# GNN block on one core: node order phase, block, graph in the column tiles, normalisation on ScalarE, and an instruction sequence of its own for the first pair

## What is computed

```
h = max(layernorm(x), 0)
hc = h transposed to (graph, feature, node)
c = relu(bn1(conv1(hc)))                  # 128x128, one tap
c = bn2(conv2(c))                         # 17 taps along the nodes
x_conv = relu(c + hc) transposed back
s = h @ w_se.T + b_se                     # 3 features per node
A = exp(-|s_n - s_m|^2) * adj
msg = relu(h @ w_msg.T + b_msg)
x_nmp = A @ msg
gi = [x_conv, x_nmp] @ w_ih.T + b_ih ; gh = h @ w_hh.T + b_hh
r, z = sigmoid(gi_r + gh_r), sigmoid(gi_z + gh_z)
n = tanh(gi_n + r * gh_n)
out = x + (1 - z) * n + z * h
```

## Time and profile before

| | |
|---|---|
| median of 3 runs | 337.67 us (337.13 to 338.13) |
| the profiled execution, its own time | 337.86 us |
| its span, first to last instruction | 336.1 us |
| mean granted TensorE clock | 0.954 |
| busy: PE, DVE, ACT, POOL | 304.8, 277.2, 152.0, 29.7 us |

### The profile page before, as it was taken

How to read it: one execution, slowest core, us unless ns; L and a number is a source line. 1 busy time by engine, 2 the same in 40 slices (tenths; PEclk the granted TensorE clock), 3 DMA queues, 4 the chain that set the end, 5 groups by cost and what they waited for, 6 DMA issues and landing times.

```text
span 336.1 us, 5716 instructions
## 1 busy us (share of the span) xinstructions
PE 304.8 (91%) x2041; PEld 278.7 (83%) x2041; DVE 277.2 (82%) x654; ACT 152.0 (45%) x250; POOL 29.7 (9%) x35
## 2 busy tenths in 40 slices
PE   5808883989999999999999999999999999999991
PEld 4708773977999899989998899889998999899880
DVE  7999977389898989898989898998989896847345
ACT  1545532446454555285426543554545652730241
POOL 5733100010001000100001000100010000000000
PEclk9865998799999999999999999999999999999995
DMA  7902100070016000700062003400140002002002
GB/s 224 188 4 38 27 2 0 25 164 2 2 29 161 1 2 0 178 12 0 3 126 65 0 3 65 124 0 2 32 96 0 0 3 62 2 1 64 0 0 64
DMA packets 52144, 14.87 MB, mean 44 GB/s; under 512 B 34548, under 2 KB 51972, under 8 KB 51988
## 3 DMA queue, kind: packets, MB, share of 16 engines
q1 hardware_dynamic: 51518, 13.18, 16.9%
q10 hardware_dynamic: 438, 1.25, 1.2%
q0 software_dynamic: 160, 0.07, 0.4%
HBM read 10.30 MB, written 4.19 MB: 43 GB/s over the span
## 4 chain that ended last, share of the span: by engine, by line
PE 77%; DVE 3%; ACT 2%; issue 1%; DVEq 0%; ACTq 0%
PE bank L886 22%; PE bank L887 21%; PE bank L888 21%; PE bank L956 3%; PE bank L983 3%; PE bank L1039 2%; PE bank L931 2%; PE bank L975 1%; PE bank L966 1%; DVE stats L533 0%; DVE place L676 0%; ACT a_hi L371 0%; ACT edge L395 0%; DVE place L687 0%; ACT a_hi L374 0%
## 5 line engine op out<-in xcount | busy, mean ns | idle before, releaser
L886 PE MATMUL bank<-a_hi,w_hi 128*128 128x256 f32 (+1 forms) x328 | 100.3, 306 | 5.7 <-DVE place L676 5.7
L887 PE MATMUL bank<-a_lo,w_hi 128*128 128x256 f32 (+1 forms) x328 | 96.8, 295 | 0.0
L888 PE MATMUL bank<-a_hi,w_lo 128*128 128x256 f32 (+1 forms) x328 | 96.7, 295 | 0.0
L886 PEld LDWEIGHTS bank<-a_hi,w_hi 128*128 128x128 f32 x328 | 64.6, 197 | 6.5 <-issue 5.9
L887 PEld LDWEIGHTS bank<-a_lo,w_hi 128*128 128x128 f32 x328 | 64.5, 197 | 0.6
L888 PEld LDWEIGHTS bank<-a_hi,w_lo 128*128 128x128 f32 x328 | 64.2, 196 | 0.0
L306 POOL TENSOR_TENSOR rstd<-var_eps,halves 128x8 f32<-128x8 f32 (+1 forms) x9 | 13.6, 1511 | 208.2 <-DVE var_eps L550 208.2
L886 PE MATMUL bank<-h_hi,w_hi 128*128 128x512 f32 (+1 forms) x66 | 26.7, 405 | 1.5 <-DVE ms_b L599 1.3
L363 ACT ACTIVATE a_f<-bank,bn_shift,bn_scale 128x512 f32<-128x512 f32 x16 | 12.5, 785 | 30.6 <-PE bank L888 28.2
L887 PE MATMUL bank<-h_lo,w_hi 128*128 128x512 f32 (+1 forms) x66 | 25.5, 386 | 0.0
L888 PE MATMUL bank<-h_hi,w_lo 128*128 128x512 f32 (+1 forms) x66 | 25.4, 385 | 0.0
(11 more groups left out here) (142 smaller groups left out, 646.2 us busy)
## 6 DMA issues: line engine op xcount, KB each, us to landing
adj_in<-in_adj SPq DMA_DIRECT2D x64, 64.0 KB, 2.3
x_slot<-in_x SPq DMA_DIRECT2D x8, 256.0 KB, 4.0
place<-in_x SPq DMA_DIRECT2D x8, 256.0 KB, 3.9
out<-x_slot SPq DMA_DIRECT2D x8, 256.0 KB, 2.6
out<-place SPq DMA_DIRECT2D x7, 256.0 KB, 2.5
place<-in_L_gnn_conv_w ACTq DMA_DIRECT2D x1, 1088.0 KB, 7.1
place<-in_L_gnn_w_ih SPq DMA_DIRECT2D x1, 384.0 KB, 4.4
out<-place SPq DMA_DIRECT2D x2, 128.0 KB, 2.3
```

What stands on the lines that cost most here:

```text
L886: pe.matmul(out, w_hi[:, mat, :], hi, start=start, stop=False)
L887: pe.matmul(out, w_hi[:, mat, :], lo, start=False, stop=False)
L888: final = pe.matmul(out, w_lo[:, mat, :], hi, start=False, stop=stop)
```

## The change

It reorders the nodes: x is loaded in four DMAs for each half pair, so that partition r*32+v holds node 4v+r, and y is stored in four. A column tile stands now phase by phase, in a phase block (v) by block, and for each block its 4 graphs. A phase of a half pair is 128 columns in a row, and a shift by one block is a shift by 4 columns for all 4 graphs. In return, what belongs to one graph is every fourth column (`by_graph`): the banks that `h_transposes` and `aggregate` write, the weights that `messages` and `out_transposes` load. The adjacency rows are loaded four times, each time whole (2 KB pieces), at offsets 0 to 3, and `adj_transposed` reads every fourth element. The columns that only a rounding to even limits took in are no longer computed. `x_normed` moves to ACT with a bias that POOL makes, and `edge` shares the space of `x_norm`. `conv_out` is cut by half pair. The differences of taps move from POOL to DVE except for the last two, copies to ACT; vectors are loaded behind the big weight on ACT's queue. The first pair has its own order on PE, ACT and DVE. The last pair's transposes by graph need both column parts. In the diff, `x_normed` and `gates` are ACT's, and `first_pair` is DVE's.

```
         def load_x(s, k):
-            sp.dma_start(x_slots[s % 4][:, k * GB:(k + 1) * GB, :], ...).then_inc(x_in[s % 4][k], 16)
+            src = x[...].rearrange("b (v r) d -> r v b d", r=4)
+            for r in range(4):
+                sp.dma_start(x_slots[s % 4][r * VN:(r + 1) * VN, k * GB:(k + 1) * GB, :], src[r]
+                             ).then_inc(x_in[s % 4][k], 16)
...
         def load_adj(s, k):
-            for i in range(N // QUAD):
-                src = adj[..., :, rows].rearrange("b (j c) a -> c b j a", c=QUAD)
-                sp.dma_start(adj_in[k][rows, :, :].rearrange("c b (j a) -> c b j a", a=QUAD), src)
+            src = adj[...].rearrange("b (c r) m -> c b (r m)", r=4)
+            for i in range(4):
+                sp.dma_start(adj_in[k][i * QUAD:(i + 1) * QUAD, :, 3 - i:3 - i + 4 * N], src)
...
         def norm_rstd(i, graphs):
             pool.tensor_tensor(rstd[:, graphs], var_eps[:, graphs], halves[:, graphs], ALU.pow)
+            pool.tensor_tensor(norm_bias[:, graphs], neg_mean[:, graphs], rstd[:, graphs], ALU.mult)
...
+            def x_normed(s, k):
+                act.wait_ge(nbias_ready, (k if s == 0 else s + 1) + 1)
+                if k == 0:
+                    wait(act, edgem_ready, 2 * s)
+                for b in range(k * GB, (k + 1) * GB):
+                    act.activation(x_norm[:, b, :], x_slots[s % 4][:, b, :], ACT.Identity,
+                                   bias=norm_bias[:, b:b + 1], scale=rstd[:, b:b + 1])
...
-                dve.transpose(adj_T[k][:, :], adj_in[k][:, :, :].rearrange("n b m -> n (b m)"))
+                dve.transpose(adj_T[k][:, :].rearrange("m (b n) -> m b n", b=GB), adj_in[k][:, :, 3:3 + 4 * N:4])
...
-                    lo = max(0, begin - shift) // 2 * 2
-                    hi = min(VN, (VN - shift + 1) // 2 * 2)
+                    lo, hi = max(0, begin - shift), min(VN, VN - shift)
...
+            def by_graph(ap):
+                return ap[:, :].rearrange("p (n b) -> p b n", b=GB)
             def h_transposes(t, k):
-                    tr = pe.transpose(bank[B_F[k]][:, b * N:(b + 1) * N], x_norm[:, k * GB + b, :], ident[:, :])
+                    tr = pe.transpose(by_graph(bank[B_F[k]])[:, b], x_norm[:, k * GB + b, :], ident[:, :])
...
                     for b in range(b0, b1):      # messages
-                                      h_f[p][:, b * N:(b + 1) * N], w_ms[:, :], start=True, stop=True)
+                                      by_graph(h_f[p][:, half(b // GB)])[:, b % GB], w_ms[:, :], ...)
...
             def distances(t, k):
-                pe.wait_ge(msb_ready, 3 * t + 3 - k)
+                if t == 1:
+                    pe.wait_ge(b_added, 1)
+                    pe.wait_ge(convf_ready, 4)
...
+            def gates(s):
+                gate_r(s, 0)
+                gate_z(s, 0)
+                x_normed(s + 2, 0)
+                gate_n(s, 0)
+                x_normed(s + 2, 1)
+                hh_n_half(s, 1)
...
+            def first_pair():
...
+                vector_columns()
+                odd_differences(0)
+                first_differences()
+                norm_columns()
+                second_differences()
+                h_low(0, 0)
+                weights_low(1)
+                h_low(0, 1)
+                weights_low(2)
+                messages(0)
+                phase_sums(0)
+                weights_low(3)
+                dist_sides(0)
+                a1_low_sums(0)
...
```

More of the change, by code:

```diff
@@ L467, in iteration @@
                     h_copies(t, 1)
[L468 to L473 removed]
+                gate_n(s - 1, 1)
+                g_scaled(s)
                 if ahead:
@@ L496, in iteration @@
                     nmp_high(t, 1)
-                gate_r(s, 0)
-                gate_z(s, 0)
-                gate_n(s, 0)
-                hh_n_half(s, 1)
-            for s in range(NP):
+                gates(s)
+            first_pair()
+            gates(0)
+            nmp_high(1, 0)
+            nmp_high(1, 1)
+            for s in range(1, NP):
                 iteration(s)
@@ L686, in conv_out @@
                     dve.wait_ge(comb_f, 2)
[L687 to L688 removed]
+                to = conv_f[:, half(k)].rearrange("p (q e w) -> p e q w", q=2, e=2)[:, e]
+                product, rest = (ap.rearrange("p (q k w) -> p k q w", q=2, k=2)[:, k]
+                                 for ap in (bank[B_CB][:, :], pre[e]))
+                dve.scalar_tensor_tensor(to, product, bn_scale[:, 1:2], rest, ALU.mult, ALU.add
+                                         ).then_inc(convf_ready, 1)
             def conv_low(s, k):
@@ L852, in iteration @@
                 if ahead:
-                    a1_low(t)
+                    a1_low_sums(t)
+                    a1_low_phases(t)
                     nmp_low(t, 1)
-                n_hidden(s, 0)
-                n_argument(s, 0)
-                z_times_h(s, 0)
-                if s + 2 < NP:
-                    x_normed(s + 2, 0)
-                z_times_n(s, 0)
-                gates_out(s, 0)
-                if s + 2 < NP:
-                    x_normed(s + 2, 1)
-            for s in range(NP):
+                gates(s)
+            first_pair()
+            gates(0)
+            nmp_low(1, 0)
+            nmp_low(1, 1)
+            for s in range(1, NP):
                 iteration(s)
@@ L1097, in _ @@
-            pe.transpose(bank[B_Z][:, 0:NVEC], vecs[:, :], ident[0:NVEC, 0:NVEC]).then_inc(vecT_done, 1)
-            h_transposes(0, 1)
-            weight_transposes(1)
-            pe.wait_ge(w_ms_ready, 2)
-            messages(0)
-            split_done(1)
-            conv1(0, 0)
-            conv1(0, 1)
-            weight_transposes(2)
-            weight_transposes(3)
-            dist_transposes(0)
-            weight_transposes(4)
-            distances(0, 0)
-            distances(0, 1)
```

627 lines of the change are left out of this document (348 added, 279 removed).

## The result

The changed kernel takes 347.29 us (median of 4 runs, 346.33 to 348.06) beside 337.90 for the kernel before on the same chip (337.13 to 338.75): a ratio of 1.028, 95% interval 1.024 to 1.032. I had forecast 329.4 us and a faster kernel. The profiled execution is the one of 348.06 us, with a span of 346.1.

The account below looks back on a forecast made before the run. PE was taken to bound the iterations, with the gain to be won in the first 83 us. 337.86 - 8.8 (first pair) + 0.5 (ACT behind) - 1.3 (iterations) + 1.3 (end) gave 329.6, median 329.4; range 325 to 336.8.

Parts of the forecast that it names:

- PE's own access: PE's weight loads and bank writes at every fourth float32: taken as 0, upper bound 5.1 us a pair.
- rival (2): PE pays for loads and writes at 16-byte steps, up to 361 us; chance of slower 0.13, of 333 to 337 0.08.
- Leg 1: Startup up to the first product "g": vectors at 9.6, then 15.7 us of DVE, so "g" starts at 25.3.
- Rival (3): Startup held by data: vectors and big weight land 3 us or more later, 332.5 to 336 us; chance 0.11.
- Leg 2: Startup from "g" at 25.3 to pair 1's transposes at 41.0, through DVE, POOL's rstd and ACT's normalisation.
- Leg 3: PE's work from pair 1's transposes at 41.0, priced by columns: 15.9 us, to 56.9.
- Leg 4: Gates of pair 0, up to pair 2's first transpose: at 74.6, where it was 83.43 before.
- Iterations: Pairs bound by PE: fewer columns save 0.18 us a pair, 1.3 over seven pairs; 35.5 us from iteration to iteration.
- ACT's cover for the normalisation: In the iterations ACT takes 2.0 us more, hidden ahead of hh_n; without cover each pair pays up to 2 us.
- The end: Last results and stores: transposes wait for both parts (0.4), eight issues at 0.26 or less; 1.3 us more.
- The startup: The first pair, up to pair 2's first transpose: 8.8 us shorter than before, 74.6 where it was 83.43.

Follow-up runs that it names:

- e1: The changed kernel, but messages loads 128 neighbouring columns of h_f as weights and not every fourth: 332.99 us, ratio 0.983.
- e2: The kernel before, but messages loads every fourth column of h_f (16 bytes apart) as weights: 351.07 us, ratio 1.037.
- e3: The changed kernel, but h_transposes and aggregate write their 128 columns side by side in the bank: 348.36 us, ratio 1.029.
- e6: e4 with vectors back on SP's queue behind x, ahead of the adjacency, and conv2's weights behind w_se on ACT's: 340.70 us.
- n2: Changed kernel's column order made in PSUM writes, rows in natural order, DMAs of the kernel before, extra ACT copies for messages: 333.52 us, ratio 0.985.
- n3: n2 with ACT's two copies for the messages ahead of the four others in each iteration: 334.34 us.
- e4: The changed kernel with x loaded and results stored in natural node order, one DMA per half and not four: 345.90 us.
- e8: The changed kernel with pair 1's statistics and moments earlier on DVE, and norm_rstd(2) ahead of POOL's two sums of taps: 341.53 us.
- e7: The changed kernel with 48 spare products ahead of pair 1's h_transposes and 30 ahead of pair 2's: 351.55 us, ratio 1.039.
- e5: The kernel before, but moving operands and outputs of conv2's products are one run of neighbouring columns, not 8 runs: 332.11 us, ratio 0.981.
- s2: The changed kernel, but messages loads every second column of h_f as weights, 8 bytes apart: 333.09 us.
- s8: The changed kernel, but messages loads every eighth column of h_f as weights, 32 bytes apart, over both halves: 348.97 us.

## Why the prediction was wrong, step by step

**PE's own access** is the first step that failed, and by itself it is worth more than the whole loss. I took 0, since the loads of every 17th element at half clock kept pace, and concluded that a float32 product at full clock asks no more of its load. It does: 121 ns for each of 16 messages a pair, 1.93 us, against a break-even of 55 ns on the loads alone that rival (2) named. In e1 and e2 this one load is worth 14.3 and 12.2 us. The row was of another form: a transposing load at half clock, with 0.215 us from one to the next. The transposing loads of `out_transposes` at the same step do cost almost nothing (0.90 us for 8 from start to start with what follows, 0.80 before), as the earlier trace rows had it; what I carried over to `messages` was the half clock and the form at once. At full clock it is the form that decides. Whether a product's load at this step would be hidden at half clock, no row shows. In e1's startup the sixteen messages with contiguous loads take 3.33 us at a granted clock of 0.50 to 0.58, so the load at 16 bytes brings a product at full clock to about the pace of half clock. That is the upper bound which I had written down and set aside (0.106 more for each). Rival (2) had the mechanism right for a third of its accesses; the writes, priced the same there, are free (e3). Its chances were 0.13 and 0.08.

**Leg 1**: "g" at 31.11, forecast 25.3. The vectors were transposed at 13.87 and not at 9.6, and that is 4.3 of the 5.8. Rival (3), data, was right about the vectors and about the adjacency, which costs them 1.4 to 2.0 us (10.70 in e6, 8.67 and 9.32 in n2 and n3, which load all but the adjacency alike). It was wrong about the big weight, which landed 5.7 us behind its issue at 1.64, earlier than before (7.1 behind 2.41), and neither it nor my sum had x in it. SP's form of the x loads put the first statistics at 8.28 and not at 3.85, and both, x and vectors, had to be mended to see it (e4, e6). The other 1.5 us are in DVE's sum: from the vectors to "g" it took 17.2 us where I had 15.7, with DVE waiting 1.3 for ACT's conv1 results. In n2, without that wait, it took 16.7. That "g" starts there at 25.38, as I had forecast, is luck: the vectors came 0.9 us earlier than I took.

**Leg 2**: from "g" to pair 1's transposes 18.5 us, forecast 15.7. DVE's two transpositions at 16-byte steps took 2.09 as priced (2.1), and side by side 1.29 in n2, so the excess was the 0.8 that I took. `x_norm` took 3.18 for eight, not 2.0, for its price came from a copy that reads a bank. That is 1.2. `rstd` started at 42.52, 11.4 us behind "g" where I had 10.1: DVE waited 1.4 us for ACT's first edges, which my sum lacks. e8 shows that this order, more than any price, made the stall.

**Leg 3**: 19.5 us, forecast 15.9. The difference is 1.9 for messages (3.65 against 1.75) and 1.7 for the half clock behind the stall, which I left out: transposes and "a0" took 4.60 where I had 2.9, and 2.60 in e7 at full clock. **Leg 4**: 19.1, forecast 17.7, with `x_norm` at 0.40 (1.2 for eight) the likely part, which no run isolates.

**Iterations**: forecast 35.5, measured 36.2. Without the strided load 34.3 (e1), so the gain was larger than my 0.2: 1.4 us, of which runs of columns give 0.9 (e5) and fewer columns my 0.18; some 0.3 stays unexplained. ACT's cover for the normalisation held: no wait for it in the iterations.

**The end**: 1.8 us, forecast 1.3. The issues cost 0.45 us each, not 0.26; that was the price of a load of one 0.5 KB row.

Put together: in e1, without the strided load, the time is 333, inside the range, but partly by luck. Pair 2's transposes stand there at 85.58, 11.0 us behind my 74.6. What follows them takes 246.9 us, where my sum has 253.2, so a gain of 6.3 that I had not counted hides more than half of what the startup lost. **The startup** is thus the second step that failed: I had it 8.8 us shorter than before, and it was 4.8 longer, 2.2 in e1. The loads and the order held it (legs 1 and 2). It is also enough to turn the sign. With the strided load still in it, the changed kernel loses 6.6 us by e6 and 5.8 by e8. If the two add up, which no run shows, it stands at 335, below the kernel before.

## What to carry to other kernels

Price a memory access by a row of the same instruction form at the same clock, or leave the range open to both ends of it: a transposing load at a wide step is cheap where the load of a float32 product doubles. A permutation is free here in the PSUM writes, and is paid for in weight loads of float32 products, in DMA issues and in copies with permuted writes; count the copies that a new order forces before its gains. Attribute a gain to its part: the fastest version here wins ahead of pair 2's transposes, and nothing in the iterations, for which the nodes were reordered. In a startup, list all loads that one instruction waits for, with their queues; mending one of two that are equally late shows nothing. A sum that comes out right can hold two errors that cancel; compare it leg by leg.

## What the runs showed of the hardware

- A float32 product's weight load of 128 columns takes 190 ns at 4 bytes from element to element, 196 at 8, 328 at 16 and 335 at 32 (e1, s2, the changed kernel, s8). A transposing load at 16 bytes takes 210 where the contiguous one takes 141, and its successor starts only 12 to 13 ns later.
- PSUM writes of transposes and of float32 products at every fourth element cost nothing (e3: ratio 1.029 without them, 1.028 with them).
- A product of 256 columns whose moving operand and output stand in eight runs of 32 takes 12 ns more than with both in one run (e5, 294 against 282).
- SP needs 0.45 to 0.50 us for a DMA issue of x or of results, whether it carries 32, 64 or 256 KB, and 0.25 for one row of 0.5 KB.
- ACT: 128x128 from SBUF with a bias and a scale per row 0.40 us; 128x512 from PSUM written in permuted order 1.09 us, in plain order 0.6.
